# Two edits to a hand-written stage order: the MLP's third gated product ahead of the maxima, and linear attention's turned result behind the next projection

## The reference

```
x = x + attn_a(layernorm(x))      # softmax attention, 16 heads of 8
x = x + ffn(layernorm(x))         # first call
x = x + attn_b(layernorm(x))      # linear attention, 16 heads of 8
x = x + ffn(layernorm(x))         # second call
```

```
x = x + local_attention(rope(l2norm(q)), rope(l2norm(k)), v) @ wo
h = layernorm(shift(x)) * ln_g + ln_b
a, g = split(h @ w1 + b1)         # 341 columns each
x = x + (a * gelu(g)) @ w2 + b2
```

```
q, k = elu(q) + 1, elu(k) + 1
context = k^T v                   # one 8 x 8 block for each head
out = (q context) / (q sum(k) + 1e-6)
return out @ Wo + bo
```

## Time and profile before

| what | value |
|---|---|
| runs shown | 1023.16, 1024.66 and 1032.9 us; median 1024.66 |
| profiled execution, its own time | 1026.61 us |
| its span, first to last instruction | 1024.8 us |
| mean granted TensorE clock | 0.981 |
| PE busy | 954.9 us, 93% of the span |
| DVE busy | 739.1 us, 72% |
| ACT busy | 732.8 us, 72% |
| POOL busy | 383.4 us, 37% |

### The profile page before, as it was taken

The page is one execution under the profiler, slowest core; times in us unless marked ns, Lnnn a source line. Parts: engine busy times, 40 slices in busy tenths (PEclk is TensorE's granted clock), DMA queues, the critical chain, the costliest instruction groups (busy, mean ns, idle before and its releaser), DMA issues.

```text
span 1024.8 us, 22947 instructions
## 1 busy us (share of the span) xinstructions
PE 954.9 (93%) x8744; PEld 584.2 (57%) x8744; DVE 739.1 (72%) x1225; ACT 732.8 (72%) x1564; POOL 383.4 (37%) x266
## 2 busy tenths in 40 slices
PE   8999999998889999999998989989899999999985
PEld 3333333333666767667666656656576676766751
DVE  7888878883877778777775766677587787877741
ACT  3677777777778687787875766757677868787752
POOL 2110103002756545536342434334354454544500
PEclk9999999999899999999998999999999999999997
DMA  2200000001410101001000000001011001110100
GB/s 80 64 8 2 2 2 2 2 2 32 100 27 17 28 22 28 22 17 33 18 21 17 14 15 22 17 11 23 17 23 24 22 22 28 23 38 17 39 16 10
DMA packets 23303, 23.72 MB, mean 23 GB/s; under 512 B 8626, under 2 KB 15068, under 8 KB 23196
## 3 DMA queue, kind: packets, MB, share of 16 engines
q1 hardware_dynamic: 23196, 22.27, 9.2%
HBM read 6.16 MB, written 1.05 MB: 7 GB/s over the span
## 4 chain that ended last, share of the span: by engine, by line
PE 62%; DVE 8%; ACT 2%; issue 2%; POOL 1%; DVEq 0%; POOLq 0%
PE psum L1287 8%; PE psum L1256 5%; PE psum L1217 5%; PE psum L1196 5%; PE psum L1158 5%; PE psum L1168 5%; PE psum L1206 4%; PE psum L1295 4%; PE psum L1160 4%; PE psum L1159 4%; PE psum L1280 3%; PE psum L1229 2%; PE psum L1274 2%; PE psum L1181 2%; DVE f_PT L1550 2%
## 5 line engine op out<-in xcount | busy, mean ns | idle before, releaser
L1087 POOL TENSOR_TENSOR f_A<-f_A,f_BS 128x1024 f32<-128x1024 f32 x64 | 150.9, 2357 | 222.8 <-DVE f_BS L1526 222.6
L765 DVE TENSOR_REDUCE a_M<-psum 128x2 f32<-128x1024 f32 x128 | 155.4, 1221 | 33.9 <-PE psum L560 33.1
L1092 POOL TENSOR_TENSOR f_A<-f_A,f_RN 128x1024 f32<-128x1024 f32 x64 | 121.7, 1902 | 90.8 <-ACT f_RN L1418 86.9
L683 ACT ACTIVATE a_PT<-psum 128x1024 f32<-128x1024 f32 x128 | 128.6, 1023 | 24.9 <-PE psum L570 24.8
L1403 ACT ACTIVATE f_PW<-psum,f_NM 128x128 f32<-128x128 f32 x512 | 138.1, 380 | 4.2 <-DVE f_NM L1558 4.2
L1558 DVE TENSOR_REDUCE f_NM<-psum 128x4 f32<-128x512 f32 x128 | 82.3, 685 | 66.2 <-PE psum L1196 65.1
L1369 ACT ACTIVATE f_SQ<-psum 128x512 f32<-128x512 f32 x128 | 75.1, 608 | 70.3 <-PE psum L1160 65.8
L1522 DVE TENSOR_TENSOR f_A<-psum,cos 128x512 f32<-128x512 f32 x128 | 87.8, 686 | 44.0 <-ACT f_SQ L1369 43.9
L1217 PE MATMUL psum<-f_VS,f_PT 128*64 128x65 f32 x1024 | 81.3, 228 | 32.5 <-DVE f_hidden L1605 13.8
L1217 PEld LDWEIGHTS psum<-f_VS,f_PT 128*64 128x64 f32 x1024 | 67.8, 139 | 65.5 <-issue 48.3
L1287 PE MATMUL psum<-f_mid,f_w 128*128 128x512 f32 (+1 forms) x192 | 86.7, 602 | 2.7 <-DVE f_mid L1588 2.7
(11 more groups left out here) (196 smaller groups left out, 1939.4 us busy)
## 6 DMA issues: line engine op xcount, KB each, us to landing
f_VS<-f_V SPq DMA_DIRECT2D x112, 130.0 KB, 2.3
raw<-L_ffn_wqkv_dram SPq DMA_DIRECT2D x2, 768.0 KB, 5.4
a_XT<-L_attn_a_x_dram SPq DMA_DIRECT2D x4, 256.0 KB, 2.9
out_dram<-f_OUT SPq DMA_DIRECT2D x4, 256.0 KB, 2.3
f_w<-L_ffn_w_dram SPq DMA_DIRECT2D x2, 341.0 KB
tables<-const_dram SPq DMA_DIRECT2D x1, 512.0 KB, 4.0
f_wo<-L_ffn_wo_dram SPq DMA_DIRECT2D x8, 64.0 KB
const<-const_dram SPq DMA_DIRECT2D x1, 264.0 KB, 3.0
```

Of the source, the lines that this page charges most:

```text
L683: nc.scalar.activation(PT[:, i % 4, :, :], psum[:, pair("by_key", i), :], ACT.Exp, scale=float(DA) ** -0.5).then_inc(s("exped"), 1)
L765: nc.vector.tensor_reduce(M[:, quads % 2, t, 2 * j:2 * j + 2], psum[:, pair("scores", i), :], AX_X, ALU.max).then_inc(s("maxed"), 1)
L1087: nc.gpsimd.tensor_tensor(A[:, k % 2, :, :], A[:, k % 2, :, :], BS[:, k % 2, :, :], ALU.add)\
L1092: nc.gpsimd.tensor_tensor(x, x, RN[:, k % 2, :, None].to_broadcast([P, 2 * HW, DW]), ALU.mult)\
```

## The change

Two entries of the stage table move, and one goes.

- DVE makes the third block's gated product in the stage `w1`, right behind the first two, and the stage `w1_last` is gone. So it now stands in front of `keys_b`, the maxima (`soften`), `turn_p_2` and `tokens_b`, where it stood behind them and the layer norm's stages.
- On PE `features_b` moves from in front of `project` to behind it, and `project_b` from in front of `turn_o` to behind it. On ACT `features_b` moves from in front of `squares` to behind it. DVE's `project_b` keeps its place, behind `rope`.

```diff
 STEP = {
     "PE": [("features_a", 0, of_first), ("project_a", 1, of_first), ("latent", 8, of_sequence),
-           ("features_b", 10, of_sequence),
-           ("project", 0, of_tile), ("turn", 1, of_tile), ("context", 9, of_sequence), ("project_b", 10, of_sequence),
-           ("turn_o", 3, of_tile), ("w1", 5, of_group), ("turn_p", 2, of_tile),
+           ("project", 0, of_tile), ("features_b", 10, of_sequence), ("turn", 1, of_tile), ("context", 9, of_sequence),
+           ("turn_o", 3, of_tile), ("project_b", 10, of_sequence), ("w1", 5, of_group), ("turn_p", 2, of_tile),
...
-    "ACT": [("features_a", 0, of_first), ("latent", 8, of_sequence), ("features_b", 10, of_sequence),
-            ("squares", 0, of_tile), ("turn", 1, of_tile), ("values", 0, of_tile), ("turn_o", 3, of_tile),
+    "ACT": [("features_a", 0, of_first), ("latent", 8, of_sequence),
+            ("squares", 0, of_tile), ("features_b", 10, of_sequence), ("turn", 1, of_tile), ("values", 0, of_tile), ("turn_o", 3, of_tile),
...
     "DVE": [
...
-            ("var_b", 7, of_sequence), ("var_y", 10, of_sequence), ("w1_last", 5, of_group), ("wo", 3, of_group),
+            ("var_b", 7, of_sequence), ("var_y", 10, of_sequence), ("wo", 3, of_group),
...
-                    elif stage in ("w1", "w1_last"):
+                    elif stage == "w1":
                         layer = i // SEQS % LAYERS
-                        for blk in (0, 1) if stage == "w1" else (2,):
-                            w = HID_BLOCKS[blk][1]
+                        for blk, (_, w) in enumerate(HID_BLOCKS):
                             dve.wait_ge(s("up"), 3 * i + blk + 1)
                             dve.wait_ge(s("gated"), 3 * i + blk + 1)
```

## The result

The changed kernel takes 1011.3 us (median of 6 runs, 1011.14 to 1015.36), the kernel before, run beside it, 1026.36 us. The ratio is 0.9857, with a 95% interval of 0.9828 to 0.9886: 1.4% faster, by 15.1 us between the medians. The profiled execution took 1011.42 us (span 1009.6), 15.19 less than the profiled one of before. The forecast was 1010.1 us, a gain of 14.5.

A forecast was written before the change was run, and what follows sets the result against it. PE bounds the kernel (busy 93%), so only its pauses and their clock can give much. Profiled 1026.61 less 14.5 from four stages is 1012.1, less 1.95 for the profiled run's excess over the median: 1010.1 us; range 1007.5 to 1013.

The forecast's parts named there:

- The stall and its cause: Steps 28, 32, 36, 40: PE's second sums tile waits 3.45 us each for the bank DVE's late third product frees.
- The product costs nothing where it goes: DVE's 0.74 us product fits into idle time ahead of the maxima, in ordinary w1 steps too: cost 0.
- What is late next: PE's second sums tile then waits for copy f_PT, some 1 us; later PE waits at most about 1.3 for center_y.
- DVE's chain sets the end: DVE's queue from first maxima through sums, rope and project_b's sum sets center_y: 9.21 us each in four steps.
- the second rival: All of the stall is saved: four waits (13.8) and half-clock loss return whole, 23.8 us, giving 1000.9; chance 0.04.
- The reorder: features_b behind the projection on PE lets rope start some 1.1 us earlier a time, 4.5 us in all.
- the third rival: Projection waits for its new banks as long as features_b would for its input; 4.5 us lost, 1014.6; chance 0.05.
- the fourth (slower): Third product waits for its gate and holds back the maxima in twelve ordinary w1 groups: 1040; chance 0.02.
- The clock: PE's granted clock stays full in the four steps, since the pause left is only some 1 us.
- the first rival: Clock falls all the same in a remaining PE pause: 1020 or 1016 us; chance 0.09.
- The rivals' estimate of the half clock's loss: PE at half clock behind the pause for an estimated 5 us, losing 2.5 us of work in each of four steps.
- The sum: First maxima to center_y in the four steps falls from 51.37 to 36.84 us in all: gain 14.5.

The follow-up runs named there:

- the second edit alone: Changed kernel with the third gated product put back late on DVE, the PE and ACT reorder kept: 1025.37 us, ratio 1.0005 to the kernel before.
- the first edit: Third gated product ahead of the maxima; run alone, as the changed kernel with PE's and ACT's old order put back: 1015.95 us, ratio 0.991.
- keeping the clock up: Kernel before, with four products of constants filling PE's pause between the two sums tiles of the four steps: 1021.21 us, ratio 0.9972.
- the early copy: Changed kernel with turn_p_2 ahead of the scores on PE and its copy f_PT ahead of DVE's maxima in w1 steps: 998.2 us, ratio 0.9732.

## Why the prediction was right

- *The stall and its cause.* Right: with the product ahead of the maxima the wait for `f_hidden` is gone, and the run with the second edit alone, which leaves the product late, keeps it all four times.
- *The product costs nothing where it goes.* Right: it fits between the third `up` tile and the maxima in both kinds of steps, and the run that moves it only in four groups is equal to the change.
- *What is late next.* Right, in both places: PE waits for the copy (0.82 us, "some 1 us"), and then for DVE's X in front of `center_y` (1.13 us, "at most about 1.3"). The 1.3 is not worked out there: the times given, 557.5 and 558.12, make 0.6, and PE was done about half a microsecond before the 557.5.
- *DVE's chain sets the end.* Right, and this is the term that carries the size: 9.21 us forecast, 9.10 measured. It was shown from both sides: 0.65 us more in the chain cost 0.65 a time, and the sum into X moved forward by about 0.75 us gave 0.73. With that falls the second rival, by which the whole stall would come back (23.8 us). Of the 0.11 us that the forecast was long, 0.07 lies in DVE's `sums`, taken at 1.17 us and measured at 1.10 (552.70 to 553.80).
- *The reorder.* Right: worth 4.5 us forecast, 4.6 measured, and only behind the first edit. No wait of the projection for its new banks stands in the changed kernel's list, so the third rival falls too, and the fourth (slower) with the idle time of 0.9 us that is left in front of the maxima of an ordinary step.
- *The clock.* The forecast that two pauses of about 1 us leave it at 1.00 held in the profile of the changed kernel, so the first rival did not come about. The rule of the Trainium skill on frequent short pauses ("TensorE: Matmul & The Clock Gate", section "A second HAM failure mode: psum-queue depth-cycling") is not seen here: the clock stayed at 1.00 with pauses of 0.95 and 1.25 us in the first of the four places and equal waits in the others. The rivals' estimate of the half clock's loss, 2.5 us a time, was too large as a cost in time: keeping the clock up gave 1.2 in the order of the kernel before. In that experiment too `center_y` waits for X, so part of what PE wins is given back there.
- *The sum.* 14.5 forecast, 14.96 in the four stages: four times the 0.11 above. The rest, to 15.19, lies in the last distance and at the ends of the span, which the change does not touch. The term that did not hold is the 1.95 us taken off for the profiled execution: after the change that one is only 0.12 us above its median (1011.42 and 1011.3). So the time came out 1.2 us above the forecast although the gain was larger. The two errors have opposite signs, so it is in part luck that the time lies as near the forecast as it does.
- *What was missed* is in an expectation and not in the forecast: the early copy was to give 0.8 us a step and gave 1.19. The wait's row holds less than the pause costs (0.82 against 1.04), and the transposes gave 0.15 more.

## What to carry to other kernels

A wait that leads the list is worth no more than the chain that ends just behind it: walk each engine's queue to the next common point and take the latest. Here PE alone would have promised 23.8 us, DVE's chain said 14.5, and 15 came. When one edit takes a wait away, look for the wait that will be last then, since an edit that is worth nothing today (the reorder) may be worth nearly half of the first one's gain afterwards (4.6 and 10.4 us).

## What the runs showed of the hardware

- A wait's row undercounts a pause of PE. It books 0.82 us, but the distance of the starts shrank by 1.04 when the pause went. Without a pause a matmul starts before the one in front of it has ended (0.05 us behind its start, where it lasts 0.22), and with a pause that overlap is lost too.
- A pause of 3.45 us on PE was followed by a granted clock of 0.50; pauses of 0.95, 1.25 and 1.35 us in the changed kernel were not, even with two of them within 8 us, and neither was the pause of 1.56 us in the run with the product behind the copy (granted clock 1.00 from 270 to 960 us).
- Between kernels that share a stage, the distance between groups repeats to 0.02 us where the granted clock stays at 1.00. Where it falls, as in the four stages of the kernel before, single distances differ by up to 0.85 us. By contrast the time up to the first such product (321.7 to 323.1 us) and the last distance (28.4 to 30.9 us) move by more than a microsecond between the profiles. Small effects are better read from the distance than from the total.
